# State space stage of a two-layer perceiver block: 64 instead of 128 moving columns in the intra products

## What is computed

```python
zxbcdt = einsum('bld,ed->ble', u, W_in)
z, xBC, dt = ...
xBC = silu(causal_depthwise_conv(xBC, conv_w, conv_b))
x, Bm, Cm = ...            # x: 16 heads of 64 channels; Bm, Cm: 128 states
dt = softplus(dt + dt_bias); A = -exp(A_log)
# per token: h = h * exp(dt*A) + (dt*x) outer B ;  y = h . C
y = ssd_scan(dt, A, x, Bm, Cm) + D * x
y = y * silu(z)
y = y * rsqrt(mean(y*y) + eps) * norm_w
return einsum('ble,de->bld', y, W_out)
```

## Time and profile before

| | us |
|---|---|
| median of three executions | 1218.13 |
| lowest, highest | 1217.71, 1218.86 |
| the profiled execution, its own time | 1216.42 |
| its span, first to last instruction | 1214.7 |
| state space rounds in it (first L1914 to last L1938) | 1058.3 to 1102.5 |

### The profile page before, as it was taken

One profiled execution on the slowest core, in us unless ns is written; L12 is line 12 of the kernel. 1 busy time (PEld: TensorE's weight loads), 2 busy tenths in 40 slices (PEclk: granted clock), 3 DMA queues, 4 the chain that ended last, 5 costly groups with the idle time before them and its releaser, 6 DMA issues.

```text
span 1214.7 us, 14306 instructions
## 1 busy us (share of the span) xinstructions
PE 1060.9 (87%) x4740; PEld 494.1 (41%) x4740; DVE 853.1 (70%) x1168; ACT 473.8 (39%) x713; POOL 363.4 (30%) x170
## 2 busy tenths in 40 slices
PE   7999999699999899879438999999888779895897
PEld 3444444344444344434213444444622135464353
DVE  5577777899999155683872299999376457475795
ACT  2354454566665035135770210100034514335163
POOL 5244544244333013000011277775100020082003
PEclk9999999799999899889869899999969889998897
DMA  6154554422221693020010245455100010000000
GB/s 243 48 170 145 169 176 144 162 103 103 104 104 35 249 339 139 0 87 1 1 69 1 98 169 194 175 192 140 35 1 1 12 61 1 1 1 1 2 1 35
DMA packets 41844, 112.60 MB, mean 93 GB/s; under 512 B 4529, under 2 KB 15313, under 8 KB 35665
## 3 DMA queue, kind: packets, MB, share of 16 engines
q1 hardware_dynamic: 38608, 101.13, 23.9%
q10 hardware_dynamic: 2880, 9.96, 2.5%
q0 software_dynamic: 320, 1.05, 0.3%
HBM read 103.18 MB, written 7.34 MB: 91 GB/s over the span
## 4 chain that ended last, share of the span: by engine, by line
PE 57%; DVE 24%; issue 9%; ACT 8%; DVEq 1%; ACTq 1%; DMA 0%; POOL 0%; SPq 0%; POOLq 0%
PE PS L1502 5%; PE PS L1504 5%; PE PS L1503 5%; DVE arena L659 4%; PE PS L870 4%; PE PS L249 3%; PE PS L250 3%; PE PS L251 3%; PE PS L1570 2%; DVE XN L609 2%; DVE arena L1796 2%; DVE arena L662 2%; PE PS L1596 1%; PE PS L1487 1%; PE PS L760 1%
## 5 line engine op out<-in xcount | busy, mean ns | idle before, releaser
L714 PE MATMUL PS<-arena 128*128 128x512 f16 x256 | 97.1, 379 | 9.7 <-POOL arena L466 7.7
L744 PE MATMUL PS<-arena 128*128 128x512 f16 x256 | 97.7, 382 | 6.1 <-DVE arena L659 5.9
L491 POOL TENSOR_TENSOR arena<-arena 128x2048 f16<-128x2048 f32 x16 | 69.4, 4337 | 112.0 <-ACT arena L536 106.0
L1502 PE MATMUL PS<-arena 128*128 128x512 f16 x256 | 97.0, 379 | 1.8 <-DVE arena L1393 1.8
L745 PE MATMUL PS<-arena 128*128 128x512 f16 x256 | 97.8, 382 | 0.0
L746 PE MATMUL PS<-arena 128*128 128x512 f16 x256 | 97.7, 381 | 0.0
L715 PE MATMUL PS<-arena 128*128 128x512 f16 x256 | 97.0, 379 | 0.0
L716 PE MATMUL PS<-arena 128*128 128x512 f16 x256 | 97.0, 379 | 0.0
L1503 PE MATMUL PS<-arena 128*128 128x512 f16 x256 | 97.0, 379 | 0.0
L1504 PE MATMUL PS<-arena 128*128 128x512 f16 x256 | 97.0, 379 | 0.0
L659 DVE SCALAR_TENSOR_TENSOR arena<-arena,MASK 128x512 f16<-128x512 f16 (+1 forms) x64 | 96.0, 1499 | 0.1
(11 more groups left out here) (353 smaller groups left out, 2364.0 us busy)
## 6 DMA issues: line engine op xcount, KB each, us to landing
arena<-in_ctxT SPq DMA_DIRECT2D x32, 1024.0 KB, 6.4
arena<-in_ctx SPq DMA_DIRECT2D x16, 1024.0 KB, 5.2
arena<-in_w ACTq DMA_DIRECT2D x8, 1024.0 KB, 5.4
arena<-in_w SPq DMA_DIRECT2D x8, 1024.0 KB, 4.8
XN<-in_ffnGU SPq DMA_DIRECT2D x16, 384.0 KB, 3.4
XN<-in_WinT SPq DMA_DIRECT2D x16, 290.0 KB, 5.0
gu_hi<-arena SPq DMA_DIRECT2D x16, 192.0 KB, 3.3
gu_lo<-arena SPq DMA_DIRECT2D x16, 192.0 KB, 3.4
```

The costliest lines, as they stand in the source:

```text
L714: pe.matmul(bank, CHI[:, b, e, cols], QHI[:, e, :], start=(e == 0), stop=False)
L744: pe.matmul(PS[:, t, :], PHI[:, j, cols], CHI[:, b, j, :], start=False, stop=False)
L1502: pe.matmul(bank, QHI3[:, e, cols], CHI3[:, b, e, :], start=(e == 0), stop=False)
```

## The change

```diff
                 for h in range(SSM_H):
                     pe.wait_ge(s4_mix, 4 * q + h // 4 + 1)
-                    ins = pe.matmul(PS[:, 4 + h // 4, (h % 4) * P:(h % 4 + 1) * P], DECAY[:, h, :],
-                                    DTX[:, h * SSM_P:h * SSM_P + P], start=True, stop=True)
+                    ins = pe.matmul(PS[:, 4 + h // 4, (h % 4) * P:(h % 4) * P + SSM_P], DECAY[:, h, :],
+                                    DTX[:, h * SSM_P:(h + 1) * SSM_P], start=True, stop=True)
                 ins.then_inc(s4_intra, 1)
```

## The result

Nine executions of the changed kernel took 1219.68 to 1222.65 us, median 1221.82; nine of the kernel before, run beside them, 1216.05 to 1219.08, median 1218.86. The ratio is 1.0029 with a 95% interval of 1.0019 to 1.0039: slower by 0.3%, clear of the 0.2% that a measurement of this kernel can tell. (The quotient of the two medians alone would be 1.0024: the medians are 2.96 us apart, the means, 1221.66 and 1218.11, 3.55 us.) The profiled execution took 1222.65 us, its span is 1220.9 us, and the mean granted clock 0.926 where it was 0.931.

A forecast was written before the change was run, and what follows sets the result against it. L1938, on the chain of waits in all four rounds, was taken as paced by TensorE's weight loads. Streaming 0, end of round four -0.05, clock +2.7 made +2.65 us: 1218.13 to 1220.8 us, range 1217.6 to 1222.5.

The forecast's parts named there:

- Streaming: L1938, all rounds: fewer moving columns gain nothing, at most 0.3 us, as the weight load sets the pace; counted as 0.
- The end of round four: L1842 behind the fourth round's L1938 gets its last result sooner; 0.05 us gained.
- The clock: First round only: narrower passes after idle time bring TensorE's clock down to 1.2 GHz; +2.7 us, chance 0.53.
- The price: First round's fall: ten L1938 passes at 99 ns more, 1.0 us, plus 1.7 us for L1944; 2.7 us.
- the upper end: First round, early fall: 24 L1938 passes 2.4 us, L1944 1.7 us, and 0.3 us more; 4.4 us.
- the columns do set the pace: Rival, all 128 L1938 passes: load plus streaming in sequence, 53 ns off each, 6.8 us faster, 1211.3 us; chance 0.06.
- The idle-gap rule: TensorE over the rounds: the clock holds if no long idle gap; sum -0.05 us, 1218.1 us; holds case's chance 0.37.
- The rule of the same page: L1938: weight loads overlap matmuls in flight only on different row groups, so fewer columns would make the kernel faster.

The follow-up runs named there:

- experiment 1: Changed kernel with the first round's intra products back at 128 moving columns, 64 in the other three rounds; median 1217.56 us, ratio 0.9996 to the kernel before.
- experiment 2: Kernel before with 64 moving columns in the first round alone, 128 in the other three; median 1220.62 us, ratio 1.0021.
- experiment 3: Changed kernel plus eight unread filler matmuls in TensorE's idle time ahead of the first round's L1938; median 1217.35 us, ratio 0.9991 to the kernel before.
- experiment 4: Kernel before plus eight unread filler matmuls in the first round's idle time, as a control; median 1217.05 us, ratio 0.9995.
- experiments 10 and 11: Changed kernel again, unaltered, one profiled execution each; 1221.84 and 1219.40 us.
- experiment 7: Changed kernel with the stationary operand cut to 64 columns too, VectorE adding on 64 partitions; median 1217.81 us, ratio 1.0002 to the kernel before.
- experiment 8: experiment 7 without GpSimd's L1714 to L1716 in the second and third round; median 1212.11 us, ratio 0.9954 to the kernel before.

## Why the prediction was right

**The sign and the size.** Forecast +2.65 us on the median, 1220.8, and a range of 1217.6 to 1222.5; measured +2.96 and 1221.82. The mechanism was the one forecast, shown by experiments 1 to 4: undoing it in one round, doing it in one round, and taking away one of its two conditions, with a control. That +2.65 and +2.96 lie so near each other is partly luck: the fall itself was priced at 2.7 us and costs 4.24 in three of the four profiled executions with 64 columns (3.31 in the fourth).

**Streaming.** Forecast: no gain, since the load of 128x128 float32 weights sets the pace at 110 to 112 ns. It is 110 ns with 64 columns and 109 with 32, and 63 ns once the stationary operand is halved too. The comparison of L1555 with L244 in the trace had the answer ready.

**The end of round four.** Forecast -0.05 us; rounds two to four together are 0.05 us shorter (29.72 against 29.77).

**The clock.** Place right: in the first round, not in the others. The clock came back later than forecast, at 1076.8 us, which is 1.6 us behind the end of L1944; only the second execution of 10 and 11 has it back within L1944, at 1070.3. The price was right per pass and mis-sized in the number of passes. A pass at 1.2 GHz was put 99 ns dearer. Nine of the 32 passes start ahead of the fall, 23 behind it, and L1938 as a whole takes 2.33 us more: 101 ns a pass. But I took ten such passes (1.0 us), and 23 come nearly to the upper end (24, 2.4 us). L1944 was put at +1.7 us and is +1.79. L1914 takes 0.67 us more, and the 0.51 us of slack before L1917 covered most of it: 0.12 is left, where the upper end had 0.3. That is 2.33 + 1.79 + 0.12 = 4.24 us in all, near the upper end of 4.4. That the medians differ by less fits experiments 10 and 11: the fall is not always as early, and other stretches of 1.2 GHz come and go. I gave 0.53 to a fall that decides the median; it came in every execution that was profiled, so the lean was right and the chance low.

**A reading that was incomplete.** The lean to the fall rested on L1555 and L885, told as runs without a break. They are, but both have TensorE idle just ahead of them, which the prediction does not say:

```profile
875.28 1.04 PE L1532 MATMUL PS<-arena 96*128 96x512 f16 x4 [1.41 <-DVE arena L1428]
876.15 3.75 PE L1555 MATMUL PS<-arena 128*128 128x32 f32 x32
```

```profile
491.15 4.49 PE L885 MATMUL PS<-MEANW,arena 128*128 128x1 f32 x32 [1.60 <-ACT arena L824]
```

L244, which held, is longer and wider both. So these rows could not tell narrow passes by themselves from narrow passes behind idle time; experiments 3 and 4 did, for 64 columns. The rows were a nearer likeness of the first round (1.44 us idle, then narrow passes) than the prediction says.

**What was wrong in the reasoning.** "So whatever a pass of L1938 gains or loses counts in full: 128 passes, nothing beside them." For the loss it held in the first round: 4.12 of the 4.24 us are L1938 and L1944. For a gain it did not: experiment 7 took 1.56 us off L1938 in the second round and 0.26 us off the round, for the most part because VectorE's L1853 then meets GpSimd's L1716, which ends 0.13 us ahead of it in the kernel before. The chain of waits names what ended last, not what would end last 0.2 us sooner. The rival "the columns do set the pace" was priced at 6.8 us on that sentence; experiment 7, with a gain per pass of about the same size (110 to 63 ns), brought nothing in the median, so it would have brought much less.

**Two rules that pointed elsewhere.** The idle-gap rule of the Trainium skill ("TensorE: Matmul & The Clock Gate", section "Why this matters for your kernels") would have given no change. The idle time ahead of the first L1938 is 1.44 us in both kernels, and the clock falls in one. The rule of the same page, section "The mechanism", that weight loads overlap matmuls in flight only for differing row groups, would have given a faster kernel. At 64 columns and 110 ns a pass the loads still cover L1938 in full (17.2 us beside 17.2), all with all rows, so the trace does not bear it out. (The same section of the Trainium skill also lets a load run ahead of matmuls when it aims at the background weight buffer; read with that, it gives no such forecast.)

## What to carry to other kernels

Before narrowing a float32 matmul's moving operand, look for a row of the trace with the same stationary shape and fewer columns: if its pace is the same, the columns are free, and taking them away gains nothing and may cost. Read the granted clock beside the busy time, since TensorE's row is full in both cases, and ask of each narrow run what stands just before it: idle time followed by narrow passes is what costs here, and filling the idle time or widening those passes, a quarter of all, mends it. And do not price a gain from the chain alone; look at what ends a little earlier on the other engines.

## What had not been expected of the hardware

Two instructions that never met before the change of experiment 7 met there, and the later one was held up: VectorE's L1853, 1.22 us alone, took 2.32 us where it began while GpSimd's L1716 was running, and ended 1.08 us after it. L1716 took 2.13 us, as in the kernel before. With L1716 left out L1853 took 1.22 us again, in experiment 8. Both read and write SBUF only; VectorE's L1849, which reads PSUM too, began at 1079.04 beside the same L1716 and took 1.22 us.

The clock fell in the third and fourth round of experiment 7 behind 2.18 and 1.96 us of idle TensorE, although what followed the idle time were full passes of 512 columns (L1933) and no narrow ones. Behind 1.07 or 1.08 us at the same place it held, in the kernel before as in experiment 8, which has the same operands on TensorE as experiment 7. So a delay of 1.1 us on another engine cost a second time, through the clock: L1933 of the third round took 3.40 us instead of 1.98. Filling only this idle time was not tried.
